# The start of the second block: image 1's combination and its q, k are moved around and into image 0's local attention, with the one-hot lists in two buffers

## The chip, the core and the metric

One core of one Trainium2 chip runs the whole program in one launch. Times are device microseconds (us). "The profile" is one execution taken by the hardware profiler; its times count from the start of its span.

## What is computed

The input is x, eight images of 16 x 16 tokens with 192 channels, 2048 tokens in all. Two blocks follow each other, each an attention and a mixture of experts. Cut to what matters here:

```
x = x + NeighbourhoodAttention(ln(x))                 # 12 heads of 16, 7x7 window
t = x as tokens
t = t + MoE0(ln(t))   # 32 experts, 6 a token, at most 48 tokens an expert; plus a shared expert
x = t
x = x + FullAttention(ln(x)) over one row of 16 tokens # 12 heads, bias; "local"
t = x as tokens
u = ln(t)
h = u + CausalAttention(rms(u) * w1)   # 256 tokens an image, 12 q heads, 3 kv heads, rotary
t = t + h + MoE1(rms(h) * w2)          # 16 experts, 2 a token
```

The routed part of MoE0 is worked out per expert slot, not per token: for each pair of experts 128 slot rows with 192 channels. To add it to the tokens, the kernel multiplies one-hot matrices (which slot row belongs to which token) with these rows. This is "the combination".

## The kernel before

**Layout.** A tile has 128 tokens on 128 partitions; an image is two tiles (t = 0, 1). x stays in SBUF as `x_all` from start to end. Most other buffers are views of one large tensor `R`, so the same words serve the first block, the start of the second and the last expert stage at different times. There are eight PSUM banks of 512 words: S0, S1, T0, T1, O0, O1, M0, M1. Engines run their own instruction streams in a fixed order, and every hand-over is a semaphore: `s("name")` counts for the stage, `await_(engine, WINDOW, "qkv", i, k)` waits for the k-th event of that name of the local attention of image i.

**Stages.** (1) For each image: neighbourhood attention, router and shared expert of block 0. (2) The routed experts of block 0: eight rounds (`jj`) of two expert pairs, with their weights streamed through a ring of five buffers. The end of a round's down projection counts `b_y`. Its 128 x 192 results are kept as three bf16 parts in `y0_all`. (3) The stage that the change touches, here called the second block: for image i the combination, layer norm, local attention (`WINDOW`), then rms norm, causal attention (`CAUSAL`) and the router of block 1. (4) Routed experts of block 1, and the output.

**The second block's order.** It is software-pipelined over images and written out by hand, in a function pair per engine: `c_window(i)` holds the local attention of image i+1 with causal projections of image i around it, `c_causal(i)` the causal attention of image i with the local projections of image i+2. The loop runs `for i in range(-1, B)`. Fillers are put in numbered slots: `extra` on TensorE (`fill(u)` after the scores of group u, `(u, "transposed")` after the transposes, "weighted" before the second denominators, "turned" before the output's transposes), `between` on VectorE, `before` on ScalarE. There is no planner.

**One local attention.** Six groups of four heads (three per tile). For a group: TensorE makes the scores (line 594 mask, 597) in banks S0, S1, M0 in turn; VectorE takes the negated maximum (714); ScalarE the exponentials (743); TensorE transposes them (614) into T0 or T1; VectorE (687) or ScalarE (752) copies them to SBUF; TensorE multiplies with v (636) into O0 (tile 0) or O1 (tile 1). ScalarE then copies the sums (732), TensorE turns them back (644), VectorE divides by the denominators (704, 705), TensorE transposes the result into M0 (666), ScalarE copies (759), and TensorE projects (678); VectorE adds the result to x (1609).

**In front of it.** q and k are needed in a split form. After TensorE's q, k (line 808) and v (815), VectorE adds the bias (828, 839) and `split_qk` writes q and k as bf16 parts (539, 556, 557, 542, 543) and sets these in place (547 to 554), eleven instructions in six steps; TensorE transposes the parts in six groups (569) into S0, T0, S1, T1, O0, O1 and ScalarE (766) and VectorE (775) copy them to `qkT`.

**The combination.** `c_comb` (TensorE, 1967) does 2 tiles x 16 pairs x 3 parts = 96 matmuls an image into M1. Its one-hot matrices come from POOL: `c_onehot(i, t)` writes 16 matrices for one tile (1057) to `comb_s`, a single buffer of 2 tiles, and moves the ids on (1061). VectorE's `combine` adds M1 to x (1452) and takes the layer norm's statistics (868, 871); POOL works out 1/sqrt (`w_root`, 1009, 1010), VectorE's `w_norm` applies it (876), TensorE's `w_head` transposes the result (794) and ScalarE copies it to `headT` (799).

**At the begin.** In front of the loop: combination 0, its norm, q, k, v, split and transposes. In `c_window(-1)`: attention 0, with combination 1 in slots 1 to 3, `w_norm` and `w_head` of image 1 near its end. In `c_causal(-1)`: q, k, v of image 1, layer norm (`normed`, 876) and rms norm (`rms`, 1473, with ScalarE's squares, 1168, and two roots of POOL) of image 0, `c_head(0)`, then split and all transposes of image 1. In `c_window(0)`: attention 1, with `causal_qkv(0)` (1993) in slot 1 and combination 2, ScalarE's `c_raw` (1175) and VectorE's `rotate` (1495 to 1504).

POOL: lists of image 0 (needed ids are there long before), w_root(0), lists of image 1, and in the loop the roots and the lists two images ahead.

## Time and profile before

| | |
|---|---|
| median of 3 runs | 1249.82 us (1249.12 to 1258.29) |
| the profiled execution | 1249.4 us, its span 1247.3 us |
| TensorE busy | 1023.5 us, 82% of the span |
| VectorE busy | 739.1 us, 59% |
| ScalarE busy | 492.8 us, 40% |
| POOL busy | 322.3 us, 26% |
| mean granted TensorE clock | 0.954 |

The span is the time from the first to the last instruction of the profiled execution. Busy time is the sum over an engine's instructions; the share is an average over four stages with different limits, so it says little about this one. The granted clock is a share of full speed, 2.4 GHz; it takes the values 1.00 and 0.50 (1.2 GHz), and a mean lies between them. In rows of a timeline the first number is the start, the second the length of the whole piece (for several instructions from the first start to the last end), and the brackets tell how long the engine was idle in front of it and whose end released it. PE is TensorE, PEld its weight loads, DVE VectorE, ACT ScalarE, POOL GpSimd.

### The profile page before, as it was taken

How to read it: one execution, taken by the hardware profiler on the slowest of the kernel's cores; microseconds unless marked ns; L12 is line 12 of the kernel's file. 1: busy time of each engine (PE TensorE's matmuls, PEld its weight loads, DVE VectorE, ACT ScalarE, POOL GpSimd, SP SyncE). 2: the span in 40 equal slices, each digit the busy share in tenths (PEclk: the TensorE clock that was granted, in tenths of full speed). 3: DMA queues.
4: the chain of work that ended last, by engine and by line, in shares of the span. 5: the costliest groups of instructions: out<-in, count | busy, mean ns of one | idle time of the engine just before them, and what ended most of it. 6: DMA issues, size and time to landing. Idle time of an engine off the chain costs nothing.

```text
span 1247.3 us, 26074 instructions
## 1 busy us (share of the span) xinstructions
PE 1023.5 (82%) x9535; PEld 799.4 (64%) x9574; DVE 739.1 (59%) x2287; ACT 492.8 (40%) x1225; POOL 322.3 (26%) x516
## 2 busy tenths in 40 slices
PE   4899999999998799675888878787876668988891
PEld 3677776776776455464666657575664447888891
DVE  6586586686674244254577777777766675332334
ACT  1452452553543222032465455555554553212110
POOL 0000000000000640167444463636101213222331
PEclk8999999999998899987999999999998989999996
DMA  9152241341341999200000000000000027788875
GB/s 351 28 144 72 72 143 54 89 143 34 109 143 56 295 405 415 60 1 1 1 2 1 19 1 19 1 19 2 18 2 18 18 89 272 269 275 288 289 260 168
DMA packets 69045, 144.80 MB, mean 116 GB/s; under 512 B 4896, under 2 KB 55360, under 8 KB 66656
## 3 DMA queue, kind: packets, MB, share of 16 engines
q1 hardware_dynamic: 64352, 132.88, 31.6%
q0 software_dynamic: 4608, 10.79, 2.6%
q8 instruction: 53, 0.87, 0.3%
q14 instruction: 32, 0.26, 0.1%
HBM read 97.35 MB, written 46.30 MB: 115 GB/s over the span
## 4 chain that ended last, share of the span: by engine, by line
PE 39%; DVE 27%; issue 19%; ACT 6%; POOL 5%; DMA 4%; POOLq 0%; DVEq 0%; ACTq 0%; SPq 0%
DVE neg_max L714 5%; PE bank L1830 4%; PE bank L569 3%; PE bank L614 3%; PE bank L636 3%; PE bank L1967 3%; PE bank L1858 2%; PE bank L808 2%; PE bank L678 2%; DVE R L687 2%; DMA R<-in_ffn_gu 2%; PE bank L815 2%; POOL sorted_x L1069 2%; PE bank L1917 2%; ACT R L743 1%
## 5 line engine op out<-in xcount | busy, mean ns | idle before, releaser
L743 ACT ACTIVATE R<-bank,neg_max 128x128 f32<-128x128 f32 (+2 forms) x576 | 188.7, 403 | 143.8 <-DVE neg_max L714 143.7
L1057 POOL TENSOR_SCALAR R<-cf,ids_rel 128x128 bf16<-128x128 f32 x256 | 170.1, 681 | 0.3
L614 PE MATMUL bank<-cf,R 128*128 128x128 f32 x864 | 136.6, 282 | 28.9 <-ACT R L752 15.2
L714 DVE TENSOR_REDUCE neg_max<-bank 128x2 f32<-128x352 f32 (+2 forms) x216 | 129.9, 608 | 31.1 <-PE bank L597 25.5
L614 PEld LDWEIGHTS bank<-cf,R 128*128 128x128 f32 x864 | 96.6, 144 | 47.4 <-ACT R L743 33.1
L1009 POOL TENSOR_TENSOR rstd<-mean_var,cf 128x2 f32<-128x2 f32 x24 | 4.7, 194 | 461.1 <-DVE mean_var L871 461.1
L766 ACT ACTIVATE R<-bank 128x1024 bf16<-128x1024 bf16 x72 | 70.5, 1020 | 78.9 <-PE bank L569 78.5
L1830 PE MATMUL bank<-R 64*116 64x256 f32 (+1 forms) x512 | 97.8, 399 | 0.0
L569 PE MATMUL bank<-cb,R 128*128 128x128 bf16 x1008 | 70.6, 234 | 28.9 <-DVE R L554 28.8
L569 PEld LDWEIGHTS bank<-cb,R 128*128 128x128 bf16 x1008 | 65.3, 106 | 36.6 <-DVE R L554 27.3
L2098 PE MATMUL bank<-xsT,R 128*128 128x128 f32 x576 | 72.4, 279 | 19.8 <-DMA R<-in_ffn_w 19.3
L2098 PEld LDWEIGHTS bank<-xsT,R 128*128 128x128 f32 x576 | 68.3, 192 | 23.3 <-DMA R<-in_ffn_w 18.5
L1830 PEld LDWEIGHTS bank<-R 64*116 64x116 f32 (+1 forms) x512 | 65.4, 180 | 26.3 <-issue 16.0
L597 PE MATMUL bank<-R 128*128 128x128 bf16 (+2 forms) x576 | 77.6, 238 | 4.1 <-issue 2.4
L1234 ACT ACTIVATE R<-bank 128x384 f32<-128x384 f32 x48 | 23.5, 490 | 141.3 <-PE bank L2105 136.0
L752 ACT ACTIVATE R<-bank 128x512 f32<-128x512 f32 (+2 forms) x152 | 64.7, 463 | 17.4 <-PE bank L614 17.4
L1967 PE MATMUL bank<-R 128*128 128x192 bf16 x768 | 67.0, 246 | 2.6 <-DVE R L1434 2.6
L597 PEld LDWEIGHTS bank<-R 128*128 128x128 bf16 x576 | 51.1, 99 | 23.5 <-issue 1.3
L1967 PEld LDWEIGHTS bank<-R 128*128 128x128 bf16 x768 | 63.3, 98 | 4.2 <-DVE R L1434 3.0
L594 PE MATMUL bank<-cb 128*128 128x352 bf16 (+1 forms) x177 | 62.2, 352 | 0.7 <-ACT R L766 0.3
L636 PE MATMUL bank<-R 128*32 128x128 f32 x1152 | 50.8, 284 | 13.9 <-ACT R L752 13.4
L1734 DVE TENSOR_TENSOR R<-R,bank 128x384 f32<-128x384 f32 x48 | 26.6, 555 | 52.1 <-ACT R L1234 49.6
(258 smaller groups left out, 1940.9 us busy)
## 6 DMA issues: line engine op xcount, KB each, us to landing
R<-in_ffn_w SPq DMA_DIRECT2D x48, 864.0 KB, 6.7
sorted_x<-cmp SPq DMA_DIRECT2D x8, 4128.0 KB, 15.9
R<-in_ffn_gu SPq DMA_DIRECT2D x16, 1392.0 KB, 21.0
R<-in_ffn_dn SPq DMA_DIRECT2D x16, 768.0 KB, 17.8
xs_words<-sorted_x SPq DMA_DIRECT2D x48, 129.0 KB, 4.0
R<-token_y SPq DMA_DIRECT2D x8, 384.0 KB, 6.0
rows<-R SPq DMA_DIRECT2D x8, 224.0 KB, 2.3
out_x<-x_all SPq DMA_DIRECT2D x16, 96.0 KB, 2.4
```

What stands on the lines that cost most here:

```text
L569: ins = nc.tensor.transpose(bank[:, :].bitcast(BF16)[:, (h * 2 + t) * P:(h * 2 + t + 1) * P], qk_parts[:, row, :, :].rearrange("p s e -> p ...
L597: ins = nc.tensor.matmul(bank[:, g * kw:(g + 1) * kw], q_ap(h, t), k_ap(a, h, k0, kw), start=False, stop=(g == len(heads) - 1))
L614: ins = nc.tensor.transpose(PT[u % 2][:, at + g * P:at + (g + 1) * P], probs[:, u % 3, g * kw + c0:g * kw + c0 + P], ident)
L636: ins = nc.tensor.matmul(OB[t][j * HV:(j + 1) * HV, col:col + P], v_ap(a, h, vt), probsT[:, u % 4, at + g * P:at + (g + 1) * P], start=(k ...
L714: nc.vector.tensor_reduce(neg_max[:, u % 4, 0:g], score_bank(a, u)[:, 0:g * kw].rearrange("p (g k) -> p g k", g=g), AX, ALU.max, negate=Tr ...
L743: ins = nc.scalar.activation(probs[:, u % 3, g * kw:(g + 1) * kw], score_bank(a, u)[:, g * kw:(g + 1) * kw], ACT.Exp, bias=neg_max[:, u % ...
L752: copies_pt(lambda dst, src: nc.scalar.activation(dst, src, ACT.Copy), a, v).then_inc(psem("pta"), 1)
L766: nc.scalar.activation(qkT[:, h0:h0 + heads, :].rearrange("p h t -> p (h t)"), bank[:, :].bitcast(BF16)[:, 0:heads * 256], ACT.Copy, scale ...
L1057: ins = nc.gpsimd.tensor_scalar(comb_s[:, t, j, :], cst("iota_tok"), ids_rel[:, j:j + 1], None, ALU.is_equal)
L1830: ins = nc.tensor.matmul(GATE[g % 3][part][0:DP0, c * 256:(c + 1) * 256], wsgu[rows, 2 if k else part, at:at + DP0], xnT_all[rows, k, :], ...
L1967: ins = nc.tensor.matmul(M1[:, t * C:(t + 1) * C], comb_s[:, t, j, :], y0_all[:, j, k, :], start=(j == 0 and k == 0), stop=(j == NPAIR - 1 ...
L2098: nc.tensor.matmul(GU[r][part][:, c * P:(c + 1) * P], w[:, part * FF + c * P:part * FF + (c + 1) * P], xsT[:, r, 0, :], start=(c == 0), st ...
```

## The change

- `comb_s` becomes a list of two buffers: the old one for even images, a new one in the words behind `mT` for odd images. Those words belong to ring buffer 1 of block 0's experts, so POOL waits for `b_y` 6 before it writes there. POOL then makes the lists of image 1 before `w_root(0)`, follows with `w_root(1)`, and both halves of image 2's lists before image 0's other roots.
- In front of the loop TensorE does combination 1 into T1 in three pieces (48, 12 and 36 matmuls), and transposes image 1's norm into M1 behind image 0's transposes. VectorE puts `combine(1)` in front of the last two steps of split 0 and `w_norm(1)` behind them.
- In `c_window(-1)` attention 0 gets: in slot 1 q, k of image 1 (banks M0, M1), "weighted" the first four transpose groups of image 1, "turned" v of image 1 (M1). Scores 2, which write M0, wait for VectorE to have read q, k of image 1. VectorE has the bias additions in slot 1 and the six split steps in slots 2 to 7. Attention 0 projects into M0 instead of T0.
- In `c_causal(-1)` TensorE has only the last two transpose groups of image 1; VectorE adds the projection, takes the statistics of image 0 and reads v of image 1.
- In `c_window(0)` attention 1 has combination 2 in slots 0 to 2 (the first piece behind VectorE's read of v), `c_head(0)` into O0 in slot 2, `causal_qkv(0)` in slot 3. Image 0's layer norm stands in front, its rms norm in slot 1, rotations and split in slots 5 to 8. ScalarE has the squares in slot 0, the copy of `c_head(0)` in slot 3, `c_raw(0)` in slot 4.
- For i of 1 and more only the buffer index of the lists is new.

```diff
@@ -294,7 +294,6 @@
 hT = hT_words[0:DP0, :].rearrange("p (c t) -> p c t", c=SC)
-comb_s = hT_words.bitcast(BF16).rearrange("p (t j k) -> p t j k", t=2, j=NPAIR)
@@ -342,6 +341,8 @@
 assert at <= low[0]
+comb_s = [w.bitcast(BF16).rearrange("p (t j k) -> p t j k", t=2, j=NPAIR)
+          for w in (hT_words, R[:, at:at + SC * 2 * P])]
@@ -588,8 +589,11 @@
             await_(pe, WINDOW, "read", i + 2, u)
-        if a is WINDOW and u == 2 and i > 1:
-            pe.wait_ge(s("c_u"), nth_square("h", i - 2))
+        if a is WINDOW and u == 2:
+            if i == 0:
+                await_(pe, WINDOW, "read", 1, 2)
+            else:
+                pe.wait_ge(s("c_u"), nth_square("h", i - 2) if i > 1 else nth_square("u", 0))
@@ -668,14 +672,14 @@
-def projected(a):
-    return M0 if a is CAUSAL else T0
+def projected(a, i):
+    return M0 if a is CAUSAL or a is WINDOW and i == 0 else T0
...
         for k in range(KC):
-            ins = nc.tensor.matmul(projected(a)[:, t * C:(t + 1) * C], xnT[:, k, t * P:(t + 1) * P], w[:, k, :],
+            ins = nc.tensor.matmul(projected(a, i)[:, t * C:(t + 1) * C], xnT[:, k, t * P:(t + 1) * P], w[:, k, :],
@@ -798,12 +802,15 @@
-def qk_banks(a):
-
-    return enumerate((S0, S1))
+def qk_banks(a, i):
+
+    return enumerate((M0, M1) if a is WINDOW and i == 1 else (S0, S1))
+
+def v_bank(a, i, t):
+    return M1[:, t * C:(t + 1) * C] if a is WINDOW and i == 1 else OB[t][:, 0:C]
 def conv_qk_pe(pe, a, src, w, i):
-    for t, bank in qk_banks(a):
+    for t, bank in qk_banks(a, i):
@@ -812,7 +819,7 @@
         for k in range(KC):
-            ins = nc.tensor.matmul(OB[t][:, 0:C], src[:, k, t * P:(t + 1) * P], w[:, k, 2 * C:3 * C],
+            ins = nc.tensor.matmul(v_bank(a, i, t), src[:, k, t * P:(t + 1) * P], w[:, k, 2 * C:3 * C],
@@ -823,7 +830,7 @@
     dst = qk_window if a is WINDOW else qk
-    for t, bank in qk_banks(a):
+    for t, bank in qk_banks(a, i):
@@ -832,7 +839,7 @@
     await_(dve, a, "qkv", i, 3)
-    parts = [(P, 0, O0[:, 0:C]), (P, 1, O1[:, 0:C])]
+    parts = [(P, t, v_bank(a, i, t)) for t in range(2)]
@@ -1054,7 +1061,7 @@
         for j in range(NPAIR):
-            ins = nc.gpsimd.tensor_scalar(comb_s[:, t, j, :], cst("iota_tok"), ids_rel[:, j:j + 1], None,
+            ins = nc.gpsimd.tensor_scalar(comb_s[i % 2][:, t, j, :], cst("iota_tok"), ids_rel[:, j:j + 1], None,
@@ -1071,21 +1078,25 @@
         c_onehot(0, t)
-    w_root(0)
+    pool.wait_ge(s("b_y"), 6)
     for t in range(2):
         c_onehot(1, t)
+    w_root(0)
+    w_root(1)
     pool.wait_ge(s("zeroed"), 16 * (B + 1))
...
             c_root("h", i - 1)
-        if i + 2 < B:
+        if 0 <= i < B - 2:
             w_root(i + 2)
...
             c_onehot(i + 3, 0)
+        if i < 0:
+            c_onehot(i + 3, 1)
         if i + 1 < B:
...
             c_root("u", i + 1)
-        if i + 3 < B:
+        if 0 <= i < B - 3:
@@ -1152,11 +1163,11 @@
         act.wait_ge(s("w_xT"), m + 1)
-        copy_pair(headT, S0).then_inc(s("w_xTc"), 1)
+        copy_pair(headT, M1 if m == 1 else S0).then_inc(s("w_xTc"), 1)
...
         act.wait_ge(s("c_xT"), m + 1)
-        copy_pair(xcT, M0).then_inc(s("c_xTc"), 1)
+        copy_pair(xcT, M0 if m else O0).then_inc(s("c_xTc"), 1)
@@ -1197,8 +1208,16 @@
         run(qk_copies_act(act, WINDOW, i + 1)[2 if i >= 0 else 0:])
+        if i < 0:
+            w_head(1)
+            attention_act(act, WINDOW, 0, turned=lambda: run(qk_copies_act(act, WINDOW, 1)[:2]))
+            return
         before = {}
-        if i >= 0:
+        if i == 0:
+            before[0] = lambda: squares("u", 0)
+            before[3] = lambda: c_head(0)
+            before[4] = lambda: c_raw(0)
+        else:
@@ -1206,19 +1225,16 @@
     def c_causal(i):
+        if i < 0:
+            return
         steps = qk_copies_act(act, WINDOW, i + 2) if i + 2 < B else []
...
             before[4] = lambda: router(i - 1)
-        if i >= 0:
-            attention_act(act, CAUSAL, i, before, (lambda: c_head(i + 1)) if i + 1 < B else (lambda: None),
-                          lambda: run(steps[:2]))
-        else:
-            squares("u", 0)
-            c_head(0)
-            run(steps[:2])
+        attention_act(act, CAUSAL, i, before, (lambda: c_head(i + 1)) if i + 1 < B else (lambda: None),
+                      lambda: run(steps[:2]))
@@ -1449,7 +1465,7 @@
         dve.wait_ge(s("c_comb"), 2 * m + 2)
-        link(nc.vector.tensor_tensor(image_x(m), image_x(m), two(M1[:, 0:2 * C]), ALU.add))
+        link(nc.vector.tensor_tensor(image_x(m), image_x(m), two((T1 if m == 1 else M1)[:, 0:2 * C]), ALU.add))
@@ -1573,6 +1589,16 @@
             run(qk_copies_dve(dve, WINDOW, i + 1)[2 if i >= 0 else 0:])
+        if i < 0:
+            steps = split_qk(WINDOW, 1, link)
+            between = {k + 2: step for k, step in enumerate(steps)}
+            between[1] = lambda: conv_qk_dve(dve, WINDOW, brow, 1)
+            between[8] = lambda: add_bias(link, 0)
+            attention_dve(dve, WINDOW, 0, link, between)
+            run(qk_copies_dve(dve, WINDOW, 1)[:2])
+            return
+        if i == 0:
+            normed(0)
@@ -1594,11 +1620,11 @@
             between[5].append(lambda: w_norm(i + 2))
-        if i >= 0:
-            between[1].append(lambda: rotate(i, 0))
-            between[2].append(lambda: rotate(i, 1))
-            for k, n in ((4, 0), (5, 1), (6, 2), (7, 3), (8, 4), (8, 5)):
-                between[k].append(split[n])
+        if i == 0:
+            between[1].append(lambda: rms(0, "u", 0, xn, "c_xn"))
+        at = (1, 2, 4, 5, 6, 7, 8, 8) if i else (5, 6, 6, 6, 7, 7, 8, 8)
+        for k, step in zip(at, [lambda: rotate(i, 0), lambda: rotate(i, 1)] + split):
+            between[k].append(step)
@@ -1606,19 +1632,17 @@
             await_(dve, WINDOW, "proj", i + 1, 1)
-            link(nc.vector.tensor_tensor(image_x(i + 1), image_x(i + 1), two(T0[:, 0:2 * C]), ALU.add))
+            link(nc.vector.tensor_tensor(image_x(i + 1), image_x(i + 1),
+                                         two(projected(WINDOW, i + 1)[:, 0:2 * C]), ALU.add))
+        if i < 0:
+            ln_stats(link, 0, s("c_var"))
+            conv_v_dve(dve, WINDOW, brow, 1)
+            return
         split, copies = [], []
...
             split, copies = split_qk(WINDOW, i + 2, link), qk_copies_dve(dve, WINDOW, i + 2)
-        if i < 0:
-            ln_stats(link, 0, s("c_var"))
-            normed(0)
-            rms(0, "u", 0, xn, "c_xn")
-            run(split)
-            run(copies[:2])
-            return
@@ -1716,7 +1740,11 @@
     conv_v_dve(dve, WINDOW, brow, 0)
-    run(split_qk(WINDOW, 0, link))
+    steps = split_qk(WINDOW, 0, link)
+    run(steps[:4])
+    combine(1)
+    run(steps[4:])
+    w_norm(1)
@@ -1957,25 +1985,25 @@
     pe.wait_ge(s("wf_loaded"), 16 * 4)
-    def c_comb(i, n0, n1):
+    def c_comb(i, n0, n1, bank=M1):
...
             for k in range(3):
-                ins = nc.tensor.matmul(M1[:, t * C:(t + 1) * C], comb_s[:, t, j, :], y0_all[:, j, k, :],
+                ins = nc.tensor.matmul(bank[:, t * C:(t + 1) * C], comb_s[i % 2][:, t, j, :], y0_all[:, j, k, :],
                                        start=(j == 0 and k == 0), stop=(j == NPAIR - 1 and k == 2))
...
-    def w_head(m):
+    def w_head(m, bank=S0):
         pe.wait_ge(s("w_xn"), m + 1)
-        transpose_pair(pe, xw, S0).then_inc(s("w_xT"), 1)
-
-    def c_head(m):
+        transpose_pair(pe, xw, bank).then_inc(s("w_xT"), 1)
+
+    def c_head(m, bank=M0):
         pe.wait_ge(s("c_xn"), m + 1)
-        transpose_pair(pe, xn, M0).then_inc(s("c_xT"), 1)
+        transpose_pair(pe, xn, bank).then_inc(s("c_xT"), 1)
@@ -2021,16 +2049,37 @@
             pe.wait_ge(s("c_slots"), i - 1)
+        if i < 0:
+            def ahead():
+                pe.wait_ge(s("w_xTc"), 2)
+                conv_qk_pe(pe, WINDOW, headT, wqkv, 1)
+            attention_pe(pe, WINDOW, 0, {1: ahead, "weighted": lambda: transpose_qk(pe, WINDOW, 1, n1=4),
+                                         "turned": lambda: conv_v_pe(pe, WINDOW, headT, wqkv, 1)})
+            project(pe, WINDOW, wproj, 0)
+            return
         extra = {}
...
         def piece(k):
-            if k == 1 and i >= 0:
+            if k == 1 and i:
                 causal_qkv(i)
...
                 c_comb(i + 2, (k - 1) * n, k * n if k < 3 else 2 * NPAIR)
-        for k in range(1, 4):
-            extra[k] = lambda k=k: piece(k)
+
+        def first_head():
+            piece(3)
+            await_(pe, WINDOW, "qkTa", 1, 3)
+            await_(pe, WINDOW, "qkTd", 1, 3)
+            c_head(0, O0)
+
+        def first_piece():
+            await_(pe, WINDOW, "v", 1, 1)
+            piece(1)
+        if i == 0:
+            extra.update({0: first_piece, 1: lambda: piece(2), 2: first_head, 3: lambda: causal_qkv(0)})
+        else:
+            for k in range(1, 4):
+                extra[k] = lambda k=k: piece(k)
@@ -2045,20 +2094,16 @@
     def c_causal(i):
-        if i >= 0:
-            transpose_qk(pe, CAUSAL, i, n0=3)
+        if i < 0:
+            transpose_qk(pe, WINDOW, 1, n0=4)
+            return
+        transpose_qk(pe, CAUSAL, i, n0=3)
         if i + 2 < B:
             pe.wait_ge(s("w_xTc"), i + 3)
-            if i >= 0:
-                await_(pe, CAUSAL, "qkTa", i, 2)
+            await_(pe, CAUSAL, "qkTa", i, 2)
             conv_qk_pe(pe, WINDOW, headT, wqkv, i + 2)
-            if i >= 0:
-                await_(pe, CAUSAL, "qkTa", i, 3)
+            await_(pe, CAUSAL, "qkTa", i, 3)
             conv_v_pe(pe, WINDOW, headT, wqkv, i + 2)
-        if i < 0:
-            c_head(0)
-            transpose_qk(pe, WINDOW, 1)
-            return
@@ -2074,11 +2119,15 @@
     c_comb(0, 0, 2 * NPAIR)
+    c_comb(1, 0, NPAIR, T1)
     w_head(0)
+    c_comb(1, NPAIR, NPAIR + 4, T1)
     pe.wait_ge(s("w_xTc"), 1)
...
     conv_v_pe(pe, WINDOW, headT, wqkv, 0)
+    c_comb(1, NPAIR + 4, 2 * NPAIR, T1)
     transpose_qk(pe, WINDOW, 0)
+    w_head(1, M1)
```

## Rows read from the trace of the kernel before

**Rows 1.** Stretches: us, busy PE PEld DVE ACT POOL, clock, DMA, GB/s.
```profile
516.00:622.00 106.00, 77.69 (x725) 64.62 (x733) 50.19 (x135) 33.67 (x80) 59.47 (x95) 0.87 0.00 1
...
622.00:860.00 238.00, 191.10 (x2005) 150.99 (x2023) 172.21 (x535) 127.90 (x344) 116.13 (x182) 0.99 0.02 8
```

**Rows 2.** TensorE's timeline: start, us, line, tile, count, [idle before <- releaser].
```profile
487.72 2.82 PE L1947 MATMUL bank<-R,hTs_words 116*64 116x192 f32 x32 [0.30 <-issue]
...
516.07 8.09 PE L1967 MATMUL bank<-R 128*128 128x192 bf16 x96 [2.64 <-DVE R L1434]
...
529.13 5.49 PE L808 MATMUL bank<-wqkv,R 96*128 96x384 f32 x8 [0.68 <-ACT R L799]
...
542.25 4.55 PE L569 MATMUL bank<-cb,R 128*128 128x128 bf16 x48 [5.78 <-DVE R L554]
...
547.52 2.64 PE L1967 MATMUL bank<-R 128*128 128x192 bf16 x30
...
567.77 1.57 PE L678 MATMUL bank<-wproj,R 96*128 96x192 f32 x8 [0.68 <-ACT R L759]
```

**Rows 3.** TensorE's timeline, from image 1's q, k on.
```profile
569.18 2.74 PE L808 MATMUL bank<-wqkv,R 96*128 96x384 f32 x8
...
571.76 1.46 PE L815 MATMUL bank<-wqkv,R 96*128 96x192 f32 x8
...
584.45 5.30 PE L569 MATMUL bank<-cb,R 128*128 128x128 bf16 x48 [3.87 <-DVE R L554]
...
589.97 0.52 PE L597 MATMUL bank<-R 128*128 128x128 bf16 x4 [0.22 <-ACT R L766]
...
612.00 1.40 PE L569 MATMUL bank<-cb,R 128*128 128x128 bf16 x22 [1.74 <-DVE R L554]
...
639.28 1.96 PE L569 MATMUL bank<-cb,R 128*128 128x128 bf16 x32
```

**Rows 4.** POOL's timeline: three halves of the one-hot lists.
```profile
431.90 9.91 POOL L1057 TENSOR_SCALAR R<-cf,ids_rel 128x128 bf16<-128x128 f32 x16
...
526.95 9.31 POOL L1057 TENSOR_SCALAR R<-cf,ids_rel 128x128 bf16<-128x128 f32 x16
...
536.65 11.70 POOL L1057 TENSOR_SCALAR R<-cf,ids_rel 128x128 bf16<-128x128 f32 x16
```

**Rows 5.** VectorE's timeline.
```profile
524.30 0.56 DVE L1452 TENSOR_TENSOR x_all<-x_all,bank 128x384 f32<-128x384 f32 x1 [8.29 <-PE bank L1967]
...
525.65 0.15 DVE L871 BATCH_NORM_AGGREGATE mean_var_w<-stats 128x2 f32<-128x6 f32 x1
...
537.05 0.61 DVE L539 CAST R<-R 128x768 bf16<-128x768 f32 x1
...
541.95 0.24 DVE L554 COPY R<-R 128x384 bf16<-128x384 bf16 x1
...
578.58 0.85 DVE L1473 SCALAR_TENSOR_TENSOR R<-R,rstd,norm_w 128x192 f32<-128x192 f32 x2 [1.91 <-POOL rstd L1010]
...
599.39 0.40 DVE L1495 TENSOR_TENSOR xs_words<-R,cf 128x240 f32<-128x240 f32 x1
...
600.92 0.68 DVE L714 TENSOR_REDUCE neg_max<-bank 128x4 f32<-128x512 f32 x1
```

**Rows 6.** Busy time by stretch: two stretches with TensorE at the lower clock.
```profile
529.00:534.70 5.70, 5.57 (x9) 3.15 (x10) 0.60 (x2) 0.08 (x1) 5.70 (x11) 0.50 0.00 0
...
584.40:590.00 5.60, 5.33 (x49) 5.28 (x51) 1.59 (x3) 3.07 (x3) 5.60 (x11) 0.50 0.01 3
```

**Rows 7.** ScalarE's timeline.
```profile
547.43 1.28 ACT L743 ACT_TABLE_LOAD   x1
...
548.73 2.17 ACT L743 ACTIVATE R<-bank,neg_max 128x128 f32<-128x128 f32 x8
...
576.71 0.36 ACT L1168 ACTIVATE h_words<-R 128x192 f32<-128x192 f32 x1 [8.99 <-DVE scratch L1463]
```

**Rows 8.** Busy time by stretch: second half of attention 1.
```profile
599.39:611.96 12.57, 9.32 (x118) 6.93 (x116) 10.53 (x36) 6.34 (x18) 8.05 (x12) 1.00 0.00 1
```

## The prediction

> **What bounds the kernel now.** I read the profile in this order: the stages (busy time by stretch), TensorE's timeline through the beginning of the second block, the timelines of the other three engines over the same stretch, and the granted clock there. From 516 to 622 us the first number to see is the DMA share of 0.00 and a granted clock of 0.87, against 0.99 in the steady part that follows [rows 1]: no transfer counts here, and TensorE is both idle and slowed. TensorE's rows say why. The combination of image 0 is one run of 96 matmuls, 8.09 us; then TensorE waits for image 0's normalisation, multiplies q, k at half clock, waits 5.78 us for the split, and only then attention 0 begins [rows 2]. Behind attention 0's projection comes a second such stair for image 1: q, k, v, then a norm, a root, squares, another root, four transposes and a split with TensorE mostly idle (3.87 us of it in front of the next transposes), 48 transposes at half clock, and attention 1's scores at 589.97 [rows 3]. So the stretch is bound by a chain that hops between engines, each with little to do. The last mark I use is 612.00, where the 22 transposes of causal image 0 start: from there on instruction order and buffers are the same in both kernels as far as I can follow them, so what is won by that point is what is won at the end.
>
> **Part 1, in front of attention 0.** Image 1's combination needs its lists. POOL may build them once the sixth down projection ends, 487.72 + 2.82 = 490.5 [rows 2]. A half took 9.91, 9.31 and, beside VectorE's split, 11.70 us [rows 4]; two halves end between 509.6 and 514.3. They are wanted at 524.2, and POOL's first root behind the statistics of 525.8 [rows 5]: 11 us of cover, cost nothing. If the cover went (lists over 30 us) image 0's norm would slip by the excess. The rows show the contention on POOL's side: the same 16 instructions took 2.39 us longer beside VectorE. On VectorE's side I take 0 and leave up to 0.5 us to the range, since the lists end before the first block's last sums. The Trainium skill (GPSIMD Engine Reference, section 1, Specifications) says that GpSimd shares its SBUF interfaces with VectorE, with contention when VectorE reads two SBUF inputs or runs in a two-port mode; by that rule the lists, moved beside the end of the first block, could lengthen its chain, and the sum would be 1234.2 where by the rows it is 1233.7.
>
> TensorE now does 48 matmuls of image 1 at 8.09/96 = 0.0843 us each (4.05) while image 0 is normalised, 12 beside ScalarE's copy, 36 behind v. Image 0's transposes start at 528.2 rather than 527.8, so the path pays 0.5, and the 12 cost another 0.4. But the engine is not idle before q, k: in the old kernel they ran at 0.50 [rows 6] and took 5.49 us, while at the upper level the same eight take 2.74 [rows 2, 3]. v ends at 533.6, not 536.5. VectorE's split (first and last row at 537.05 and 541.95, eleven instructions, 5.1 us [rows 5]) now has image 1's combination inside: from the sum at 524.30 to the end of the last statistic, 525.65 + 0.15, are 1.5 us. That gives the split's end at 541.0 against 542.2. TensorE idles from 536.6 to 541.0. After 5.78 us of idle the clock was low and the 48 transposes took 4.55, with the rise inside them; wholly low they take 5.3 (48 x 0.111 from 40 of them in 4.46), at the upper level 3.0 (32 in 1.96) [rows 2, 3]. I take a fall again: the idle time is of the size that made it fall before. Transposes end at 546.2, image 1's four at 546.6, and the scores start there, against 546.9: part 1 by itself brings 0.3 us (1.8 with the clock up).
>
> **Part 2, attention 0.** Removed: 96 matmuls between the scores, 7.9 us of TensorE (30 in 2.64 as drawn [rows 2]). Added in their place: image 1's q, k into M0 and M1 (2.6 us, at 547.5 to 550.1, behind the table load of 1.28 us and beside the first exponentials [rows 7]). Scores 2 now wait for VectorE's two reads (0.56 each), so for 550.7 (the reads are set at the 0.56 of the sum, which is as wide), and end at 551.2; before they stood behind 30 of the removed matmuls, at 547.52 + 2.5, and ended at 550.5. That is a new wait, and scores 3 and all exponentials from 2 on are queued behind it, but it comes only 0.7 us behind what it replaces. After it VectorE sets the pace: six maxima (0.68 [rows 5]), three copies of as many columns (set at the same), 5.1 us of split; ScalarE's exponentials (1.1 a group, 2.17 for two) come second. Stepping through both queues in order I get the third exponential group at 553.0, the fifth at 556.3, the sixth at 558.1, the last weighted sum at 560.8. Then "weighted" puts 32 transposes (1.96) in front of the denominators, and "turned" v (1.46 as drawn, 1.3 apart) in front of the output's transposes; both lie on the path, 3.3 us. The projection, 1.57 [rows 2], ends at 567.25 against 569.3.
>
> **Part 3, between the attentions.** Before: 569.3 to 589.97 = 20.6 us. After: q, k, v, split and four of six transpose groups are done. TensorE does the last 16 transposes (1.0) and starts scores 1 at 568.35. Image 0's sum, statistics, root, norm, squares, second root and rms norm, which ended at 579.4 [rows 5], are put under scores and combination. This part gains 19.5 us. It is where the change pays.
>
> **Part 4, attention 1.** Before: 589.97 to 612.00 = 22.0 us, with causal q, k, v in front of the combination. Now image 2's 96 combination matmuls (8.1) run at slots 0 to 2: the first third waits for VectorE to have read v out of M1 (569.4), the third ends at 578.25. In their cover: norm 0 to 570.8, squares 0.8 [rows 7], a root (set at 1.0), rms by 573.9. Late next is c_head: transposes 0.45, ScalarE's copy 0.6, causal q, k, v (set at 2.0 from the eight matmuls of q, k, whose operand is a third wider [rows 3]), and behind it transposes 1, c_raw, weighted sum 0 at 583.8. From maximum 4 at 584.3 VectorE is the bound, without a pause. What it has to do then is what it did from 599.39 to 611.96, 10.53 us busy [rows 8], less a maximum (0.68) and the combination's sum and statistics (1.5), plus a second rotation (599.39 to 600.92, 1.5) and some 0.5 us between instructions: 10.4 us, so 594.8. The part takes 26.4, 4.4 more than before. Sum at the mark: 612.0 - 594.8 = 17.2 us (0.3 + 1.8 + 19.5 - 4.4).
>
> **The clock again.** TensorE is idle from 590.45 to 594.8 where it was idle 1.74 us before [rows 3]. At the upper level nothing is lost. If it falls, transposes, denominators, projection and q, k of image 2 pay; a stretch at the lower level lasted such that q, k alone lost 2.75 [rows 2, 3], and 5.33 us of busy TensorE stayed at 0.50 at 584.4 to 590.0 [rows 6]. Bounds 0 and 8.5 (all of 8.5 us of work up to image 2's v doubled); nearest is the stretch with a like idle time, some 1.5 to 3. I take 1.5. Gain 17.2 - 1.5 = 15.7.
>
> **The rest costs nothing.** The second list buffer lets POOL build image 2's lists from 540.3 to 563.6 at worst, before the root at 568.8 that is queued behind them; image 3's first half, 583.2 to 594.7, ends before the next root is wanted at about 606. SP's queue has no edit. x, banks and waits for i of 1 or more keep their order.
>
> **Sum.** The profiled execution took 1249.4 us, its span 1247.3 and 2.1 around it; the median of the three runs is 1249.82, 0.4 above. 1249.4 - 15.7 = 1233.7.
>
> **Rivals.**
> *A, as above*: gain 12.5 to 19, 1230.5 to 1237, chance 0.66.
> *B, the clock and the hops take more*: the new idle time in attention 1 costs up to 8.5 instead of 1.5, or the merged queues slip by half a microsecond at each of a dozen hand-overs. Gain 7 to 12: 1237.5 to 1242.5, point 1240. For it: busy TensorE stayed low in [rows 6]. Against: much of TensorE's work there has VectorE's beside it. Chance 0.17.
> *C, the clock never falls* in front of attention 0 or in attention 1: 1.5 + 1.5 more, 1229 to 1230.5. Chance 0.07.
> *D, it does not reach the end*: POOL or a later buffer holds the steady part at its old times. POOL would need to be late, and with 116 of 238 us busy in the steady part [rows 1] it is not. 1248 to 1251, chance 0.05.
> *E, slower*: the clock falls in the idle time before attention 0 and, with the engine busy in short pieces, does not come back before 612's work. From 516 to 622 TensorE is busy 77.7 us [rows 1], some 45 of them behind that point at full clock; doubled, with a third covered, that is 30 us more against 17 to 20 won: about 1262. It decides from 16 us of extra work on the path. For it: TensorE busy through 5.33 us and still at 0.50 [rows 6]. Against: behind the idle 5.78 us of [rows 2] the clock did come back, and the new stretch is denser. Chance 0.05.
>
> The chances follow: a measurement of this kernel can tell about 1%, 12.5 us, so faster means below 1237.3: A and C less a small tail, 0.71; same is B and D and the tail, 0.23; slower 0.06. The range leaves out D, E and the tail of B: 1229 to 1242.
>
> **What would show it.** Right: scores of attention 0 about where they were; the granted clock 1.00 under image 0's q, k; attention 1's scores within 2 us of 568; VectorE without idle time in the last 10 us before the causal transposes, these at about 595; every later mark earlier by the same amount. Wrong: scores 2 of attention 0 later than 552 (the new wait costs), attention 1 over 28 us, a clock of 0.50 past 600, or a gain at the mark that shrinks behind it.

## The result, and the profile after

Four timed executions of the changed kernel took 1234.78 to 1242.91 us, median 1239.54; four of the kernel before had a median of 1250.12. The medians differ by 10.6 us, 0.8%. The ratio on record is 0.9892 (1.1%) with a 95% interval of 0.9858 to 0.9926, which is a gain of 9 to 18 us. Forecast was a gain of 15.7, which lies inside this interval, and a time of 1233.7 us, 5.8 less than measured. The profiled execution took 1242.16 us with a span of 1240.0, 7.3 less than the span of before.

In its profiled execution the changed kernel reaches this stretch 1.6 us earlier, so I compare marks counted from the start of image 0's combination (us):

| mark | before | changed | changed, profiled again |
|---|---|---|---|
| scores, attention 0 | 30.79 | 31.64 | 30.42 |
| projection, attention 0 | 51.70 | 51.18 | 49.89 |
| scores, attention 1 | 73.90 | 53.70 | 52.40 |
| causal transposes | 95.93 | 80.77 | 80.46 |
| projection, attention 1 | 99.60 | 86.08 | 85.62 |
| causal scores | 105.61 | 95.24 | 91.63 |
| from there to the end of the span | 625.6 | 630.3 | 627.2 |

The same stretches as in [rows 1], after the change (busy PE, PEld, DVE, ACT, POOL, then clock, DMA share, GB/s); the third is the one in front of image 0's q, k and under them, the last the one behind the causal transposes:

```profile
516.00:622.00 106.00, 85.02 (x791) 69.78 (x797) 60.35 (x159) 42.58 (x109) 44.87 (x74) 0.89 0.00 1
622.00:860.00 238.00, 191.11 (x1982) 151.62 (x2000) 170.28 (x538) 125.54 (x335) 116.79 (x184) 0.98 0.02 8
524.40:533.50 9.10, 9.10 (x81) 7.96 (x79) 3.19 (x11) 0.59 (x1) 0.92 (x2) 1.00 0.00 0
595.30:607.00 11.70, 10.66 (x50) 8.42 (x51) 1.99 (x5) 3.67 (x4) 0.00 (x0) 0.50 0.01 1
```

TensorE is busier over the same 106 us. It runs without a pause and at the upper level where the old kernel multiplied q, k at 0.50 [rows 6]. But a new stretch at 0.50 stands behind 595.3, where the old kernel had none.

TensorE's timeline of the changed kernel (start, us, line, tile, count, idle before and releaser), to be held against [rows 2, 3]:

```profile
514.51 13.71 PE L1995 MATMUL bank<-R 128*128 128x192 bf16 x144 [2.64 <-DVE R L1450]
...
529.49 2.77 PE L815 MATMUL bank<-wqkv,R 96*128 96x384 f32 x8
...
540.31 5.30 PE L570 MATMUL bank<-cb,R 128*128 128x128 bf16 x48 [3.78 <-DVE R L555]
...
546.82 2.81 PE L815 MATMUL bank<-wqkv,R 96*128 96x384 f32 x8
550.37 0.38 PE L598 MATMUL bank<-cb 128*128 128x512 bf16 x1 [0.74 <-DVE R L835]
...
565.69 1.57 PE L682 MATMUL bank<-wproj,R 96*128 96x192 f32 x8 [0.68 <-ACT R L763]
567.10 1.06 PE L570 MATMUL bank<-cb,R 128*128 128x128 bf16 x16
568.21 0.39 PE L601 MATMUL bank<-R 128*128 128x128 bf16 x4
569.36 2.65 PE L1995 MATMUL bank<-R 128*128 128x192 bf16 x30 [0.76 <-DVE R L846]
...
583.60 0.43 PE L640 MATMUL bank<-R 128*32 128x128 f32 x8 [1.49 <-ACT R L1186]
...
595.28 2.53 PE L570 MATMUL bank<-cb,R 128*128 128x128 bf16 x22 [4.28 <-DVE R L555]
...
600.59 2.93 PE L682 MATMUL bank<-wproj,R 96*128 96x192 f32 x8 [0.68 <-ACT R L763]
603.31 1.06 PE L570 MATMUL bank<-cb,R 128*128 128x128 bf16 x8
604.16 4.22 PE L815 MATMUL bank<-wqkv,R 96*128 96x384 f32 x8
```

From the projection at 565.69 to attention 1's scores are 2.5 us, where before there were 22.2 [rows 2, 3]. Attention 1 takes longer, since causal image 0 now runs inside it, and is followed by 4.28 us of idle TensorE. What follows this (22 transposes 2.53 against 1.40, projection 2.93 against 1.57, q, k 4.22) is the same work at half speed.

One loss lies ahead of the moved work and is in no term of the forecast. The first 4 us of the combinations ran largely at the lower level:

```profile
514.51:516.51 2.00, 2.00 (x15) 1.92 (x16) 0.00 (x0) 0.00 (x0) 0.00 (x0) 0.59 0.00 0
516.51:518.51 2.00, 2.00 (x16) 1.91 (x15) 0.00 (x0) 0.00 (x0) 0.00 (x0) 0.56 0.00 0
```

The 144 matmuls took 13.71 us; in two of the runs below the same 144 stayed at the upper level and took 12.05. The old kernel's 96 took 8.09 in [rows 2] and 9.72 in the profile of another version of it (below, "the kernel before, filled"). Of the thirteen profiles of this document nine have this fall behind the same 2.64 us of idle TensorE and four have not, and the old kernel's order has one of each, so nothing here says that the change causes it. All marks are counted from the combination's start: up to 1.7 us between two profiles can be this fall and not an edit.

VectorE at the end of attention 1, from its maximum 4 to the end of the split, without idle time in between:

```profile
584.60 0.69 DVE L718 TENSOR_REDUCE neg_max<-bank 128x4 f32<-128x512 f32 x1 [2.66 <-PE bank L601]
...
595.04 0.18 DVE L555 COPY R<-R 128x96 bf16<-128x96 bf16 x1
```

POOL's timeline, the one-hot lists in front of attention 0 and beside it (compare [rows 4]):

```profile
490.70 9.93 POOL L1064 TENSOR_SCALAR R<-cf,ids_rel 128x128 bf16<-128x128 f32 x16 [38.30 <-PE bank L1975]
...
501.02 10.21 POOL L1064 TENSOR_SCALAR R<-cf,ids_rel 128x128 bf16<-128x128 f32 x16
...
539.92 9.50 POOL L1064 TENSOR_SCALAR R<-cf,ids_rel 128x128 bf16<-128x128 f32 x16
...
549.81 11.73 POOL L1064 TENSOR_SCALAR R<-cf,ids_rel 128x128 bf16<-128x128 f32 x16
```

Image 1's lists end at 511.2, 15 us before POOL's next root. Here are two VectorE operations of the first block's last sums that run beside them, and then the same two in the kernel before, without lists:

```profile
491.55 0.61 DVE L1448 TENSOR_TENSOR y_f<-y_f,R 128x384 f32<-128x384 f32 x1
492.19 0.41 DVE L1449 CAST R<-y_f 128x384 bf16<-128x384 f32 x1
```

```profile
491.57 0.56 DVE L1432 TENSOR_TENSOR y_f<-y_f,R 128x384 f32<-128x384 f32 x1
492.17 0.36 DVE L1433 CAST R<-y_f 128x384 bf16<-128x384 f32 x1
```

Each is 0.05 us longer beside the lists. Over the first block's last sums as a whole no loss could be told from the spread. The Trainium skill (GPSIMD Engine Reference, section 1, Specifications) says that GpSimd's SBUF interfaces are shared with VectorE, with contention when VectorE's instruction has two SBUF inputs or runs in a two-port mode. The trace agrees in direction, and for these two operations the size is a tenth of a microsecond.

### The profile page after: what moved, and what is told of

Same layout as the page of the kernel before. It is cut to its first block, busy times and chain, and to the rows that moved or that the text cites. A ratio compares the mean times of both kernels' runs of the same rounds, so it can differ in the third digit from the quotient of the medians.

```text
span 1240.0 us, 26078 instructions
## 1 busy us (share of the span) xinstructions
PE 1031.3 (83%) x9536; PEld 806.5 (65%) x9574; DVE 738.5 (60%) x2287; ACT 494.0 (40%) x1225; POOL 320.9 (26%) x516
## 4 chain that ended last, share of the span: by engine, by line
PE 39%; DVE 27%; issue 19%; ACT 6%; POOL 4%; DMA 4%; POOLq 0%; DVEq 0%; ACTq 0%; SPq 0%
DVE neg_max L718 5%; PE bank L1858 4%; PE bank L570 3%; PE bank L618 3%; PE bank L640 3%; PE bank L682 2%; PE bank L1995 2%; PE bank L1886 2%; PE bank L815 2%; DVE R L691 2%; PE bank L822 2%; POOL sorted_x L1076 2%; DMA R<-in_ffn_gu 2%; PE bank L1945 2%; ACT R L747 2%
## 5 line engine op out<-in xcount | busy, mean ns | idle before, releaser
L618 PE MATMUL bank<-cf,R 128*128 128x128 f32 x864 | 137.8, 283 | 27.7 <-ACT R L756 15.2
L770 ACT ACTIVATE R<-bank 128x1024 bf16<-128x1024 bf16 x72 | 70.5, 1020 | 78.7 <-PE bank L570 78.3
L2147 PEld LDWEIGHTS bank<-xsT,R 128*128 128x128 f32 x576 | 69.5, 194 | 24.3 <-DMA R<-in_ffn_w 19.7
```

The costliest lines, as they stand in the source:

```text
L618: ins = nc.tensor.transpose(PT[u % 2][:, at + g * P:at + (g + 1) * P], probs[:, u % 3, g * kw + c0:g * kw + c0 + P], ident)
L770: nc.scalar.activation(qkT[:, h0:h0 + heads, :].rearrange("p h t -> p (h t)"), bank[:, :].bitcast(BF16)[:, 0:heads * 256], ACT.Copy, scale ...
L2147: nc.tensor.matmul(GU[r][part][:, c * P:(c + 1) * P], w[:, part * FF + c * P:part * FF + (c + 1) * P], xsT[:, r, 0, :], start=(c == 0), st ...
```

## The experiments

Two questions were open after the result: why the gain of 15.2 us at the causal transposes was 10.4 at the causal scores and 5.7 at the end (7.3 in the span, with the 1.6 by which this execution came earlier), and which part of the change earned it. The first series is a second copy of the changed kernel for the spread, and three kernels with matmuls whose result nobody reads, only to keep TensorE's clock up.

**The changed kernel again** (no edit). 

> The changed kernel once more, unedited, for the spread. Theory (TensorE's clock decides how much of the gain is kept): the runs spread over some 8 us, 1234 to 1243, and time falls as the mean granted clock rises; median 1238 to 1241. Rival (the spread is noise of another kind): no order between time and mean clock.

Measured: six executions from 1234.47 to 1247.75, median 1240.73, ratio 0.9903 (0.9867 to 0.9940). Its profiled span was 1232.3. The marks stand in the table above: the same 80.5 us to the causal transposes, but then 11.17 us to the causal scores instead of 14.47. TensorE's timeline of this execution:

```profile
593.89 2.53 PE L570 MATMUL bank<-cb,R 128*128 128x128 bf16 x22 [4.68 <-DVE R L555]
...
599.05 1.57 PE L682 MATMUL bank<-wproj,R 96*128 96x192 f32 x8 [0.68 <-ACT R L763]
...
600.90 2.80 PE L815 MATMUL bank<-wqkv,R 96*128 96x384 f32 x8
```

The clock fell here too, but was up again for the projection. From the causal transposes to the causal scores the old kernel took 9.68 us, this execution 11.17 and the first one 14.47. So the loss behind the idle time is 1.5 us here and 4.8 there, with the same instructions.

**Late filling.** 14 unread matmuls into M1, between attention 1's last weighted sum and the causal transposes:

```
 extra["weighted"] = lambda: (
+    (warm(14, M1) if i == 0 else None),   # matmul(M1[:, 0:512], identb, mask_w[0:512]), 14 times
     transpose_qk(pe, CAUSAL, i, free, n1=3))
```

> The changed kernel with 14 matmuls of 512 columns (3.0 us, result unused) on TensorE in the idle time of attention 1, before the causal transposes. Theory (the clock that fell at 593 cost 4.5 to 5 us up to 607): the granted clock stays at 1.00 through 595 to 607, the 22 transposes start where they did, the projection of attention 1 takes 1.6 instead of 2.9 us, and the median falls by 3 to 5 us, to about 1235. Rival (VectorE's chain covers it): clock up, time within 1 us of the changed kernel.

Measured: median 1236.78 (1232.47 to 1242.81, six runs), ratio 0.9869 (0.9836 to 0.9902), 4.0 us under the changed kernel's 1240.73. Six against six executions with ranges that overlap this much do not make these 4.0 us sure, nor do the ratios' intervals.

```profile
588.23 3.19 PE L2002 MATMUL bank<-cb 128*128 128x512 bf16 x14
592.56 1.40 PE L570 MATMUL bank<-cb,R 128*128 128x128 bf16 x22 [1.14 <-DVE R L555]
...
596.23 1.57 PE L682 MATMUL bank<-wproj,R 96*128 96x192 f32 x8 [0.68 <-ACT R L763]
...
598.09 2.80 PE L815 MATMUL bank<-wqkv,R 96*128 96x384 f32 x8
```

With the idle time filled, the same transposes take 1.40 us, and causal transposes to causal scores take 9.68, exactly what they took before the change. The profiles of all runs together make the cause plain. Five have an unfilled idle time of 4.25 to 4.68 us in this place (the changed kernel twice, late lists, q, k, v behind, v early), and all five have the fall; three have it filled, and none has a fall there. The stretch to the causal scores took 14.47, 11.17, 11.32, 10.84 and 11.08 us in the five, so the fall cost 4.8 us once and 1.2 to 1.6 four times. Of the five, only the profile taken with the result stayed low past the projection. A usual fall of 1.5 us is less than the median's 4.0. Some of the rest in these profiles has another source: the causal transposes themselves stood 0.9 us earlier here (79.59) than in the second copy, as attention 1 took 27.05 us against 28.06, which the changed kernel's first profile (27.07) shows without filling.

**Filling in both places.** As above, and 14 more in front of image 0's transposes:

```
 c_comb(1, NPAIR + 4, 2 * NPAIR, T1)
+warm(14, M1)
```

> As the former, with 14 more such matmuls in the idle time before attention 0's transposes. Theory: these 48 transposes take 3.0 to 3.5 instead of 5.3 us, attention 0 starts about 1.5 us earlier (ScalarE's three copies of 1.02 us and the table load then bound it), total 1233 to 1234. Rival: the copies and the table load hide it, no more than 0.5 us.

Measured: median 1236.74 (1232.8 to 1240.09, six runs), ratio 0.987 (0.9839 to 0.9902). Attention 0's scores came at 29.10 instead of 30.59, so the 1.5 us of the forecast's "1.8 with the clock up" are there, and still there at attention 1's scores (51.04 against 52.54). Attention 1 then took 28.05 us in this profile against 27.05, one of the two lengths that the changed kernel shows without any edit, and 0.5 is left at the causal scores (88.77 against 89.27). The 1233 to 1234 expected of the median did not come, and nothing can be told from late filling alone.

**The kernel before, filled.** The unread matmuls in the old kernel's four idle places (12 in front of image 0's head, 20 in front of its transposes, 22 and 14 around image 0's causal head). 

> The kernel before with such matmuls (result unused) in its four idle times: 12 behind the combination, 20 before the transposes of image 0, 22 behind v of image 1 and 14 behind the four transposes. Theory: q, k 2.7 instead of 5.5 us, both runs of 48 transposes some 1.5 us shorter, together 6 to 7 us faster than before: 1243. So a good third of what the change brings could be had by the clock alone. Rival (the change's gain is all of the clock): this kernel comes to 1240 or below. Other rival: under 2 us.

Measured: median 1250.70 (1244.64 to 1260.72, twelve runs), ratio 0.9983 (0.9958 to 1.0007): no difference, where 6 to 7 us were expected. In its profile, which is of the slowest of the twelve executions, it had won 4.5 us by the causal transposes (91.38 against 95.93), although its combination of image 0 took 9.72 us against 8.09, and had 0.5 left at the causal scores. TensorE's timeline shows why:

```profile
606.50 1.87 PE L569 MATMUL bank<-cb,R 128*128 128x128 bf16 x22 [1.74 <-DVE R L554]
...
611.15 2.93 PE L678 MATMUL bank<-wproj,R 96*128 96x192 f32 x8 [0.68 <-ACT R L759]
...
614.73 4.18 PE L808 MATMUL bank<-wqkv,R 96*128 96x384 f32 x8
```

The clock fell after the very 1.74 us of idle time that the old kernel had there without a fall [rows 3]. So filling does not give what the change gives, and a stretch that keeps its clock once can lose it in another execution. Whether the filling in front brought this fall about, one profile can't say.

**Norm chain in front.** The second series divides the change. Here image 0's normalisation, squares, root and c_head go back in front of attention 1, as in the old kernel, and attention 1 takes its old order (combination 2 in slots 1 to 3, causal q, k, v in slot 1, rotations from slot 1). Image 1's part inside attention 0 stays. The edit, drawn together over the engines:

```
 if i < 0:
     ...
+    normed(0); rms(0, "u", 0, xn, "c_xn"); squares("u", 0); c_head(0)   # on VectorE, ScalarE and TensorE
-    if k == 1 and i:
+    if k == 1:
         causal_qkv(i)
-extra.update({0: first_piece, 1: lambda: piece(2), 2: first_head, 3: lambda: causal_qkv(0)})
+for k in range(1, 4): extra[k] = lambda k=k: piece(k)
-at = (1, 2, 4, 5, 6, 7, 8, 8) if i else (5, 6, 6, 6, 7, 7, 8, 8)
+at = (1, 2, 4, 5, 6, 7, 8, 8)
```

> The changed kernel with image 0's layer norm, squares, rms norm and c_head again in front of attention 1, and attention 1 in its old order (combination 2 in slots 1 to 3, causal q, k, v in slot 1, rotations from slot 1). q, k, v and split of image 1 stay inside attention 0. Marks count from the start of the combination of image 0. Theory (the chain costs its own 8 to 9 us in front, and the old order gives 4 to 5 back): attention 1's scores at 60 to 62 (changed kernel 52 to 54), causal transposes at 83 to 85 (80.5), so 3 to 5 us slower than the changed kernel in the begin, plus up to 3 for a clock that falls in the idle time. Rival (the hidden norm chain is where the change pays): the transposes 8 or more later. Other rival (moving it is worth nothing): within 1 us.

Measured: median 1237.76 (1233.97 to 1246.69, four runs), ratio 0.9874 (0.9821 to 0.9927). Attention 1's scores move back from 52.40 to 58.57, by 6.2 us, but the causal transposes only from 80.46 to 81.45, and the causal scores stand at 91.13, no later than in the changed kernel.

```profile
513.96 12.05 PE L1990 MATMUL bank<-R 128*128 128x192 bf16 x144 [2.64 <-DVE R L1447]
...
572.53 0.63 PE L601 MATMUL bank<-R 128*128 128x128 bf16 x4 [0.22 <-issue]
...
595.41 1.40 PE L570 MATMUL bank<-cb,R 128*128 128x128 bf16 x22 [1.88 <-DVE R L555]
```

With less put into attention 1, VectorE is not behind at its end; TensorE idles 1.88 us there, and the clock stays up in this execution. Part of the small loss is hidden by the combination, which kept its clock here (12.05 us). Counted from attention 0's scores (29.97 here) the causal transposes come at 51.5, against 50.0 and 49.1 in the two copies of the changed kernel. So hiding the chain brings 1.4 to 2.4 us at this mark, and the idle time that it makes there costs 1.5 in one copy and 4.8 in the other. The 3 to 5 us expected of it did not show: this part of the change brings nothing that the runs can tell (four executions here).

**Late lists.** POOL's root for image 0 goes in front of image 1's lists, which is where the old kernel had it:

```
+w_root(0)
-pool.wait_ge(s("b_y"), 6)
 ...                          # image 1's lists
-w_root(0)
```

> The changed kernel with POOL's lists of image 1 behind the root of image 0, where the kernel before has them; two buffers and all else stay. Theory (the early lists, which only the second buffer allows, carry the change): TensorE stands in its order before the 48 matmuls of image 1 until 536.5 and before the next 12 until about 548, attention 0 starts at 49 to 51 behind the combination's start (changed kernel 30.5 to 31.6), the causal transposes 18 to 20 us later, and the time is 1255 to 1260, slower than the kernel before. Rival (the lists are quick enough): under 3 us later.

Measured: median 1256.87 (1250.13 to 1263.7, ten runs), ratio 1.0031 (1.0007 to 1.0055), slower than the kernel before.

```profile
536.15 6.57 PE L1994 MATMUL bank<-R 128*128 128x192 bf16 x48 [12.15 <-POOL R L1064]
...
545.80 1.16 PE L1994 MATMUL bank<-R 128*128 128x192 bf16 x12 [2.64 <-POOL R L1064]
...
611.70 2.53 PE L570 MATMUL bank<-cb,R 128*128 128x128 bf16 x22 [4.28 <-DVE R L555]
...
617.01 1.57 PE L682 MATMUL bank<-wproj,R 96*128 96x192 f32 x8 [0.68 <-ACT R L763]
```

TensorE waits 12.15 us and 2.64 more, and attention 0's scores come at 46.7, 16 us later. The lists built during the first block, which only the second buffer allows, are therefore a condition of all the rest: combination 1 can only be moved ahead because of them. It also shows that a delay ahead of attention 0 reaches the end.

**q, k, v behind attention 0.** A third series was run later. In this run image 1's q, k, v, its split and all six transpose groups go back behind attention 0; the combination stays in front:

```
-attention_pe(pe, WINDOW, 0, {1: ahead, "weighted": ..., "turned": ...})
+attention_pe(pe, WINDOW, 0)
 ...
+conv_qk_pe(pe, WINDOW, headT, wqkv, 1); conv_v_pe(pe, WINDOW, headT, wqkv, 1); transpose_qk(pe, WINDOW, 1)
```

> The changed kernel with q, k, v, split and transposes of image 1 behind attention 0's projection, as in the kernel before; combination 1 and its norm stay in front of attention 0, image 0's norms inside attention 1. Theory (what pays is that q, k, v and split lie inside attention 0): attention 0 alone takes 6 to 7 us less than with them (projection at 43 to 45 behind the combination's start), but attention 1's scores come at 58 to 61 instead of 52.4 to 53.7, and the causal transposes at 85 to 88 instead of 80.5: 5 to 7 us slower than the changed kernel. Rival (the combination in front is all of it): within 2 us of the changed kernel.

Measured: median 1248.50 (1243.23 to 1250.74, ten runs), ratio 0.996 (0.9938 to 0.9983).

```profile
568.08 1.46 PE L819 MATMUL bank<-wqkv,R 96*128 96x192 f32 x8
574.90 4.70 PE L570 MATMUL bank<-cb,R 128*128 128x128 bf16 x48 [5.37 <-DVE R L555]
...
605.78 2.26 PE L570 MATMUL bank<-cb,R 128*128 128x128 bf16 x22 [4.28 <-DVE R L555]
...
610.61 1.57 PE L679 MATMUL bank<-wproj,R 96*128 96x192 f32 x8 [0.68 <-ACT R L760]
```

Attention 0 is 4.0 us shorter (from its scores at 31.69 to its projection at 47.17, 15.48 us against 19.54 and 19.47), but then TensorE idles 5.37 us for the split and runs the 48 transposes in 4.70, and the causal transposes stand at 88.86. That is 8.1 us later than in the changed kernel's first profile, whose attention 0 began at the same mark (31.64), and the median is 7.8 us higher. About two thirds of the change's gain are this move. Of the 15.2 us at the mark, some 7 (95.93 against 88.86) are left for the rest: the combination in front, with its matmuls out of attention 0, and the hidden norm chain.

**v early.** This and the next run belong to the second series and look for slack in the new order. v of image 1 is multiplied behind a group of transposes inside attention 0, while TensorE waits anyway, instead of at its end:

```
-"turned": lambda: conv_v_pe(pe, WINDOW, headT, wqkv, 1)
+(4, "transposed"): lambda: conv_v_pe(pe, WINDOW, headT, wqkv, 1)
```

VectorE reads it between its last two steps of the attention and no longer behind the projection. 

> The changed kernel with v of image 1 on TensorE in attention 0's slot 4, in front of a weighted sum that waits 1.5 us for ScalarE's copy, and VectorE's read of it before the second normalisation instead of behind the projection. Theory (v lies on the path in front of the output's transposes, and its read holds combination 2 back): attention 0's projection 1.3 us earlier (48.6 behind the combination's start, changed kernel 49.9 to 51.2), causal transposes 1.5 to 2 earlier, 79. Rival: the slot's wait was needed, weighted sums and ScalarE slip by as much; no change.

Measured: median 1238.72 (1236.33 to 1240.1, four runs), ratio 0.9864 (0.9839 to 0.9890). The causal transposes stand at 78.06, 2.4 and 2.7 us earlier than in the two copies of the changed kernel. The fall behind them is there:

```profile
599.10 2.50 PE L570 MATMUL bank<-cb,R 128*128 128x128 bf16 x22 [4.25 <-DVE R L555]
...
604.17 1.57 PE L682 MATMUL bank<-wproj,R 96*128 96x192 f32 x8 [0.68 <-ACT R L763]
```

**Spread.** In attention 1 the causal head comes at slot 1, causal q, k, v at slot 2 and the combination's last third at slot 3, so that VectorE's rotations start earlier:

```
 def first_head():
-    piece(3)
+    piece(2)
     ...
-extra.update({0: first_piece, 1: lambda: piece(2), 2: first_head, 3: lambda: causal_qkv(0)})
+extra.update({0: first_piece, 1: first_head, 2: lambda: causal_qkv(0), 3: lambda: piece(3)})
-at = (1, 2, 4, 5, 6, 7, 8, 8) if i else (5, 6, 6, 6, 7, 7, 8, 8)
+at = (1, 2, 4, 5, 6, 7, 8, 8)
-before[3] = lambda: c_head(0); before[4] = lambda: c_raw(0)     # ScalarE
+before[2] = lambda: (c_head(0), c_raw(0))
```

> The changed kernel with c_head of image 0 in slot 1 of attention 1, causal q, k, v in slot 2, the last third of the combination in slot 3, and rotations and split in their usual slots (from slot 1). Theory (VectorE has 3.2 and 2.7 us of idle time early in attention 1 and is then the bound for its last 10 us; work pulled forward shortens it): the stretch from attention 1's scores to the causal transposes falls from 27 to 28 us to 24.5, and the idle time of TensorE in front of them from 4.3 to under 2.5 us, so that the clock does not fall there. Marks: transposes at 78, causal scores at 87 to 88. Rival (c_head and q, k, v early delay the groups by the same): 27 as before.

Measured: median 1233.17 (1232.25 to 1234.54, four runs), ratio 0.9827 (0.9802 to 0.9852).

```profile
580.67 0.43 PE L640 MATMUL bank<-R 128*32 128x128 f32 x8
...
590.74 1.58 PE L570 MATMUL bank<-cb,R 128*128 128x128 bf16 x22 [1.88 <-DVE R L555]
595.11 2.92 PE L682 MATMUL bank<-wproj,R 96*128 96x192 f32 x8 [0.68 <-ACT R L763]
```

The causal transposes stand at 76.56, 3.9 us earlier than in the second copy of the changed kernel (3.7 counted from attention 0's scores). TensorE now idles only 1.88 us in front of them, and still the clock fell, against the expectation: the projection took 2.92 us, and the stretch from 590.7 to 600 was granted 0.63.

**Both, without and with filling.** The third series also has v early with spread, and the same with 14 unread matmuls in front of image 0's transposes and 5 in front of the causal ones. 

> Both edits together: v of image 1 early (run v_early) and attention 1's work pulled forward (run spread). Theory (the two lie on different stretches of the path, so they add): marks from the combination's start: projection of attention 0 at 48.6 to 49.5, causal transposes at 74.5, causal scores at 84 to 86, median about 1231 to 1232 against 1240.7 of the changed kernel. Rival (the end is set by the clock's later falls, not by the begin): the marks move, the median stays at 1233 or above.

> The same with 14 matmuls of 512 columns (result unused) in TensorE's idle time before attention 0's transposes and 5 in the one before the causal transposes. Theory: attention 0's scores at 29.1 instead of 30.4 and no fall of the clock up to the causal scores: these at 82 to 83, median 1229 to 1230. Rival (a fall of the clock avoided here comes later, as in the kernel before with such matmuls): median within 1 us of v_spread.

Measured: v early with spread 1232.67 (1229.41 to 1236.83, six runs), ratio 0.9845 (0.9813 to 0.9876), causal transposes at 75.22; with filling 1228.63 (1224.17 to 1232.1, six runs), ratio 0.9803 (0.9772 to 0.9834), at 73.95.

TensorE's timeline without filling and with it:

```profile
589.86 1.40 PE L570 MATMUL bank<-cb,R 128*128 128x128 bf16 x22 [1.88 <-DVE R L555]
...
593.53 1.57 PE L682 MATMUL bank<-wproj,R 96*128 96x192 f32 x8 [0.68 <-ACT R L763]
```

```profile
589.02 1.40 PE L570 MATMUL bank<-cb,R 128*128 128x128 bf16 x22 [0.69 <-DVE R L555]
...
592.69 1.57 PE L682 MATMUL bank<-wproj,R 96*128 96x192 f32 x8 [0.68 <-ACT R L763]
```

The two edits mostly add up at the mark (2.4 and 3.9 alone, 5.2 together). In the medians v early adds 0.5 us to spread (1233.17, 1232.67), which is not told from nothing. Attention 1 has spread's order and the same 1.88 us of idle time here, and the clock stayed up. The filled version beats both kernels: 2.0% under the one before, and 12.1 us under the changed one's 1240.7 of another series.

## Why the prediction was right in kind and, it seems, too large in size

The mechanism, rival A, is what the trace shows: a chain of hops in front of image 1 is taken off the path, and the time falls by about 1%. The size is less sure than the mechanism. The medians of the four and four executions differ by 10.6 us, outside A's 12.5 to 19 and in B's 7 to 12; the ratio makes it 13.5, inside A's; the interval of 9 to 18 holds both and the forecast's 15.7 too. With all executions (below) it is 12.0. B's mechanism was that the clock and the hops take more. In the profile taken with the result the clock did, and in the four other profiles with this idle time it did not.

- **Part 1** (forecast +0.3). Scores of attention 0 came at 31.64 and 30.42 where before they came at 30.79: minus 0.8 and plus 0.4. The upper level under image 0's q, k (2.77 us against 5.49) and the fall in front of the transposes (idle 3.78 and 3.77, then 5.30 and 4.26) came as forecast. The lists were covered. What the sum left out is the clock at the start of the combination: with the 144 matmuls in 12.05 us instead of 13.71 or 13.36 the scores came at 29.97 and 30.20 (norm chain in front, spread). The 0.5 us that the forecast gave to the Trainium skill's rule on shared SBUF interfaces were not seen; the trace has 0.05 us an operation.
- **Part 2** (+1.8). Scores to projection took 19.54 and 19.47 against 20.91, 1.4 us less. The new wait of scores 2 was forecast for 550.7 and ended at 550.37, 0.74 us long.
- **Part 3** (+19.5). Projection to scores took 2.5 against 22.2: 19.7. The size holds, but the sentence "It is where the change pays" does not: the run with the norm chain in front gave back 6.2 of them and had lost 1.0 at the causal transposes (1.4 to 2.4 counted from attention 0's scores) and nothing at the causal scores. What pays is q, k, v and the split under attention 0 (8.1 us at the mark).
- **Part 4** (-4.4). Attention 1 took 27.07 and 28.06 against 22.03, so -5.0 and -6.0. VectorE's last stretch, from maximum 4 at 584.60 to the end of the split at 595.2, was 10.6 us for a forecast of 10.4. At the mark the gain was 15.2 and 15.5 of 17.2.
- **The clock again** (-1.5). The fall came, and by the marks it cost 4.8 us in the profile taken with the result, and 1.5, 1.6, 1.2 and 1.4 in the second copy, late lists, q, k, v behind and v early. So 1.5 is what it usually costs, and the first profile is the odd one: there the clock came back only after q, k of image 2, and in the others before the projection. The bounds of 0 and 8.5 held all of them. That the usual cost was met so closely has luck in it: "nearest" was a stretch of the old kernel with transposes behind it, not this one's work.
- **The rest.** It was forecast at nothing. From the causal scores to the end took 625.6 before, and 630.3, 627.2, 632.6, 630.4 and 638.4 in the changed kernel, its second copy, late filling, filling in both places and the old kernel filled, whose instructions there are the same. The other seven profiles lie between 626.7 and 631.6. The old kernel's profile is the shortest of the thirteen, but the old kernel filled is the longest, so this is mostly spread. Falls of the clock stand in other places in each profile: from 60 to 120 us behind the causal scores the changed kernel was granted 0.94 and the one before 1.00. Whether a microsecond or two of it belongs to the change stays open.

So in the first pair of profiles the forecast's 15.7 became 10.4 at the causal scores: parts 1 to 4 brought 2.0 us less, mostly the combination's clock in part 1 and attention 1 in part 4, and the clock took 3.3 more. In the second copy it became 14.0: 1.7 less from the parts, and the clock as forecast. One slip in the forecast's own sums bears on nothing: rival C's 1229 to 1230.5 should begin from 1233.7 less 3.0, which is 1230.7.

Of its own signs of being wrong three came. The clock was 0.50 past 600, attention 1 took over 28 us in one of the two copies, and the gain at the mark shrank behind it. One sign of being right was met by luck: the causal transposes stand at 595.28 for "about 595", but this execution reached the stretch 1.6 us early, and counted from the combination's start they came at 80.77 for a forecast of 78.7.

The base was low as well. In the three series the kernel before had 46 executions from 1246.22 to 1260.03, median 1252.8. The 1249.82 of the three runs shown, and the profiled 1249.4, are from its quick side, which alone puts the forecast time some 3 us too low. Against 1252.8 the changed kernel's ten executions, median 1240.7, gain 12.0.

Open: why one execution of the same kernel gets its clock back by the projection and another only by the causal scores; and why 1.88 us of idle time ended in a fall in the profile of spread, and in none with the norm chain in front and with v early and spread together, which has the same order of work there. One execution of each can't tell a rule from chance.
